# Moving the hidden-state loads from ScalarE's DMA queue to SyncE's, and four filler matmuls instead of two

## The chip, the cores and the metric

The kernel runs on the 8 cores of one Trainium2 chip, as the same program on each core, without communication between them. The metric is the device time in microseconds of the slowest core. Engines are named as in the profile: PE is TensorE, DVE is VectorE, ACT is ScalarE, POOL is GpSimd, SP is SyncE; PEld are PE's weight loads. An engine name with a q behind it (ACTq, SPq) is that engine's sequencer, for instance while it issues a DMA.

## What is computed

A transformer layer of attention and a quantized feed-forward part on 32 sequences of 2048 tokens and width 1024, four sequences for each core:

```python
def act_quant(x):
    scale = 127.0 / jnp.clip(jnp.max(jnp.abs(x), axis=-1, keepdims=True), 1e-05)
    return jnp.clip(jnp.round(x * scale), -128, 127) / scale
...
def _L0_ffn_ref(x, w1, conv_w, conv_b, w2):      # hidden width 4096
    h = bit_linear(x, w1)                        # act_quant(x) @ ternary(w1).T
    h = depthwise_conv1d(h.transpose(0, 2, 1), conv_w, conv_b)   # 3 taps along the tokens
    h = jax.nn.silu(h.transpose(0, 2, 1))
    return bit_linear(h, w2)                     # act_quant(h) @ ternary(w2).T
...
x = _layernorm(x + _L0_attn_ref(x, Wq, Wk, Wv), axis=-1)         # causal attention, one head
x = _layernorm(x + _L0_ffn_ref(x, w1, conv_w, conv_b, w2), axis=-1)
```

The second `bit_linear` needs the largest absolute value of each token over all 4096 hidden channels before it can round any of them. So the hidden state h is written to HBM while its maxima are gathered, and read back later.

## The kernel before

Each core works through its four sequences one after the other. A sequence has these stages: load and transpose x; the V projection; attention in four blocks of 512 tokens; the first half of the feed-forward part ("FFN1"), cut into 128 chunks (4 token blocks j times 32 channel tiles c); and the second half ("FFN2"), four blocks of 512 tokens, each with 32 chunks c and an end part.

Instructions are written in program order into one stream for each engine; an engine starts an instruction only when all those before it in its stream have started, and waits on semaphores where the code says so. Such a wait holds whatever stands behind it in that stream. DMAs are written by three helpers: `Sy` puts a DMA into SP's stream, `Gp` into POOL's, `Sd` into ACT's. The common helper `_dma` deals the DMAs of one stream to four "lanes" (semaphores) in turn, and adds a wait to each DMA: the one before it in the same lane must have landed. So at most four DMAs of one stream are in flight, and a stream's DMA number k is not issued before number k-4 has landed.

**FFN1.** `emit_chunk` loads the weight tile `w1s` (SP), does 16 one-column matmuls (L498 and L503, the two border tokens) and 8 matmuls of 512 columns (L510) on PE, and then DVE copies and scales the results out of PSUM into `hsf` (L516, L519, L527). The border matmuls of the next chunk wait for L519 of this one, its main matmuls for L527. `chunk_mid` does the convolution and SiLU, `chunk_back` writes h to `hs_s` and updates the maxima (`maxb`, `negb`). Some chunks are slipped in between attention work by `pump`; the rest run as a tail after attention, by `pump(10 ** 9, dummies=True)`. Only in this tail, two filler matmuls of 64 columns (L523, L525, result never read) follow the main matmuls of each chunk in PE's stream.

**FFN2.** At the head of block j a chain of small steps turns the maxima into the scales `sbc` (the last step is the ACT copy L953). For each chunk c then:

- `ldh(c)` loads h from `hs_s` into `hsr[c % 3]`. It waits until `f2_tt(c - 3)` has read the buffer. It stands in ACT's stream.
- `f2_tt(c)` (DVE, L973) multiplies by `sbc`, `f2_magic(c)` (DVE, L978) rounds, `f2_i32(c)` (DVE, L986) converts, `f2_cast(c)` (ACT, L994) writes `hq`, of which there are three buffers.
- `f2_mm(c)` loads the weight tile `w2s[c % 4]` (SP, L1006) once the matmuls of chunk c-4 are done, and does 8 matmuls of 512 columns (PE, L1014), accumulating over c in all eight PSUM banks.

The order in which they are written decides what stands behind what:

```python
            for cp in range(3):
                ldh(cp)
            for c in range(NH + 1):
                if c < NH:
                    f2_tt(c)
                    f2_magic(c)
                    if c + 3 < NH:
                        ldh(c + 3)
                if c >= 1:
                    f2_i32(c - 1)
                    f2_cast(c - 1)
                    f2_mm(c - 1)
```

In the end part ACT and DVE split the eight banks into high and low halves (L1035, L1038), PE transposes them, DVE adds the residual `x2rd` (L1075, loaded by SP at L1054), and after the layer norm POOL stores `y` (L1097). SP's stream holds, in this order, the w2s loads of block j, its four x2rd loads, and the w2s loads of block j+1.

Of the kernel before, what the change touches and what calls it, by code (L numbers as in the profile page):

```python
# [29 lines left out]
class Prog:  # L30
# [18 lines left out]

    def op(self, eng, fn, waits=(), inc=None, inc_n=1):  # L50
        w = [(s, v) for (s, v) in self._flat(waits) if v > 0]
        if eng in self.AUTO and (inc is None or inc == self.AUTO[eng]):
            sem = self.AUTO[eng]
            idx = self.cnt.get(sem, 0) + 1
            self.cnt[sem] = idx
            chain = (sem, idx - 1)
            self.streams[eng].append((fn, w, sem, 1, chain))
            return (sem, idx)
        self.streams[eng].append((fn, w, inc, inc_n, None))
        if inc is not None:  # L60
            self.cnt[inc] = self.cnt.get(inc, 0) + inc_n
            return (inc, self.cnt[inc])
        return None
# [31 lines left out]
def build_program(T=2048, nseq=4, phases=5):  # L95
# [36 lines left out]
    identB = SB("identB", [128, 128], BF16)  # L132
# [50 lines left out]
    def AT(name, shape, dt, off):  # L183
# [45 lines left out]
               for k in range(4)]  # L229
# [22 lines left out]
    ps = es.enter_context(nc.psum_tensor("ps", [128, 4096], F32))  # L252

    NLANE = 4
    sem_names = (["tv", "vv", "sv"]
                 + [f"ld{i}" for i in range(NLANE)]
                 + [f"gd{i}" for i in range(NLANE)]
                 + [f"sd{i}" for i in range(NLANE)])
    sems = {n: es.enter_context(nc.semaphore(n)) for n in sem_names}
    P = Prog()  # L260
    _rr = {"ld": 0, "gd": 0, "sd": 0}

    def _dma(eng, queue, fn, waits):
        lane = f"{queue}{_rr[queue] % NLANE}"
        _rr[queue] += 1
        w = list(waits) + [P.tok(lane)]
        return P.op(eng, fn, w, lane, 16)

    def Sy(fn, waits=()):
        return _dma("sync", "ld", fn, waits)  # L270

    def Gp(fn, waits=()):
        return _dma("gpsimd", "gd", fn, waits)

    def Sd(fn, waits=()):
        return _dma("scalar", "sd", fn, waits)

    def Qtok(queue):
        return [P.tok(f"{queue}{i}") for i in range(NLANE)]

    def Tn(fn, waits=(), inc=None):
        return P.op("tensor", fn, waits, inc, 1)
# [39 lines left out]
    for i_m in range(ND):  # L322
        for jh in range(2):
# [3 lines left out]
            for ce in range(ND):  # L327
# [4 lines left out]
                    start=(ce == 0), stop=(ce == ND - 1)),  # L332
                    waits=wmb if ce == 0 else ())
# [7 lines left out]
               waits=[P.tok("tv")])  # L341
# [144 lines left out]
    def emit_chunk(jj, c, dummies):  # L486
        gc = gck[0]
        gck[0] += 1
        t0 = jj * 512
        stw = w1stage[gc % 3]  # L490
        hsb = hsf[gc % 2]
        ct = ctmp[gc % 2]
        wld = [g_hmm[gc - 3]] if gc >= 3 else [t_prologue_g]
        tld = Sy(lambda e, c=c, stw=stw: e.dma_start(stw[:, :], d_w1q[c]), waits=wld)
        ul = unlock_tok[jj]
        whL = [tld, ul, g_evLR.get(gc - 1)]
        for cd in range(ND):
            Tn(lambda e, cd=cd, stw=stw, t0=t0: e.matmul(  # L498
                ps[:, 3072:3073], stw[:, cd * 128:(cd + 1) * 128],
                XQ2T[:, cd * XQW + t0: cd * XQW + t0 + 1],  # L500
                start=(cd == 0), stop=(cd == ND - 1)), waits=whL if cd == 0 else ())
        for cd in range(ND):
            Tn(lambda e, cd=cd, stw=stw, t0=t0: e.matmul(  # L503
                ps[:, 3073:3074], stw[:, cd * 128:(cd + 1) * 128],
                XQ2T[:, cd * XQW + t0 + 513: cd * XQW + t0 + 514],
                start=(cd == 0), stop=(cd == ND - 1)))
        t_hLR = P.inc_last("tensor", "tv")
        wmn = [g_mainev.get(gc - 1)] if gc >= 1 else [tld, ul]
        for cd in range(ND):
            Tn(lambda e, cd=cd, stw=stw, t0=t0: e.matmul(  # L510
                ps[:, 3584:4096], stw[:, cd * 128:(cd + 1) * 128],
                XQ2T[:, cd * XQW + 1 + t0: cd * XQW + 1 + t0 + 512],
                start=(cd == 0), stop=(cd == ND - 1)),
                waits=wmn if cd == 0 else ())
        g_hmm[gc] = P.inc_last("tensor", "tv")
        Vc(lambda e, hsb=hsb, t0=t0: e.tensor_tensor(  # L516
            hsb[:, 0:1], ps[:, 3072:3073], sxinvb[:, t0:t0 + 1], OP.mult),
            waits=[t_hLR, ul, g_conv.get(gc - 2)])
        g_evLR[gc] = Vc(lambda e, hsb=hsb, t0=t0: e.tensor_tensor(  # L519
            hsb[:, 513:514], ps[:, 3073:3074], sxinvb[:, t0 + 513:t0 + 514],  # L520
            OP.mult))
        if dummies:
            Tn(lambda e: e.matmul(ps[0:64, 0:64], identB[:, 0:64], identB[:, 0:64],  # L523
                                  start=True, stop=True))
            Tn(lambda e: e.matmul(ps[0:64, 0:64], identB[:, 0:64], identB[:, 0:64],  # L525
                                  start=True, stop=True))
        g_mainev[gc] = Vc(lambda e, hsb=hsb, t0=t0: e.tensor_tensor(  # L527
            hsb[:, 1:513], ps[:, 3584:4096], sxinvb[:, 1 + t0:1 + t0 + 512],
            OP.mult), waits=[g_hmm[gc]])
        return (jj, c, gc)  # L530
# [66 lines left out]
    for s in range(nseq if phases >= 2 else 0):  # L597
# [8 lines left out]
        for i in range(NT):  # L606
# [11 lines left out]
            if i >= 2:  # L618
                wc.append(t_evac[i - 2])
            t_cast[i] = Vc(lambda e, stx=stx, stb=stb: e.tensor_copy(stb[:, :], stx[:, :]),  # L620
                           waits=wc, inc="vv")
# [4 lines left out]
            for cd in range(ND):  # L626
# [3 lines left out]
                    start=True, stop=True), waits=wts if cd == 0 else ())  # L630
# [4 lines left out]
                waits=[tt], inc="vv")  # L635
# [3 lines left out]
        if phases < 3:  # L639
            continue  # L640
        tldv = Sy(lambda e: e.dma_start(Wv2[:, :], d_wvb),
                  waits=([t_mdone, t_wvst] if s == 0 else
                         [t_prev_t, t_prev_g, t_mdone]))
        t_kdone = P.tok("sv")
        tve = {}
        for i in range(NT):
# [6 lines left out]
            for cd in range(ND):  # L653
                for h in range(2):
# [4 lines left out]
                        start=(cd == 0), stop=(cd == ND - 1)),  # L659
                        waits=wts if (cd == 0 and h == 0) else ())  # L660
# [38 lines left out]
        for sb in range(NBL):  # L699
            for ce in range(ND):  # L700
# [4 lines left out]
                for cd in range(ND):  # L705
# [4 lines left out]
                        start=(cd == 0), stop=(cd == ND - 1)),  # L710
                        waits=wts if cd == 0 else ())
# [3 lines left out]
                    waits=[tt])  # L715
# [5 lines left out]
            for iq in range(4):  # L721
                i = sb * 4 + iq
# [5 lines left out]
                for ce in range(ND):  # L728
                    for kb in range(nkb):
# [5 lines left out]
                            start=(ce == 0), stop=(ce == ND - 1)),  # L735
                            waits=wts if (ce == 0 and kb == 0) else ())
                t_s = P.inc_last("tensor", "tv")
                pro_pump(1)
                if phases >= 5 and iq % 2 == 1:
# [11 lines left out]
                    waits=[tv_m])  # L751
                tv_li = Vc(lambda e: e.reciprocal(linv[:, :], lsum[:, :]),
                           waits=[t_exp[i]])
# [139 lines left out]
        t_ldh = {}  # L893
# [4 lines left out]
        for j in range(NBL):  # L898
# [57 lines left out]
            def ldh(c):  # L956
                hb = hsr[c % 3]
                wlh = [t_spill_h[(j, c)]]
                if (j, c - 3) in t_tt2:
                    wlh.append(t_tt2[(j, c - 3)])  # L960
                elif j > 0:
                    wlh.append(t_tt2[(j - 1, NH - 3 + c)])
                else:
                    wlh.append(t_attn_t)
                    wlh.append(t_prologue_g)
                t_ldh[(j, c)] = Sd(lambda e, j=j, c=c, hb=hb: e.dma_start(
                    hb[:, :], d_hs[j, c]), waits=wlh)

            def f2_tt(c):
# [131 lines left out]
    pro_drain()  # L1101

    P.op("gpsimd", lambda e: e.nop(), waits=Qtok("gd"))
    P.op("sync", lambda e: e.nop(), waits=Qtok("ld") + Qtok("sd"))

    with es:
        with nc.Block() as block:
# [57 lines left out]
```

How the kernel before makes its waits and increments, by code:

```python
            def body(e, recs=recs, eng=eng):  # L79
                seen = {}
                for fn, waits, inc, inc_n, chain in recs:
                    for s, v in waits:
                        if v > seen.get(s, 0):
                            e.wait_ge(sems[s], v)
                            seen[s] = v
                    ins = fn(e)
                    if chain is not None and chain[1] > seen.get(chain[0], 0):
                        ins._wait_ge(sems[chain[0]], chain[1])
                        seen[chain[0]] = chain[1]
                    if inc is not None:
                        ins.then_inc(sems[inc], inc_n)
```

## Time and profile before

| | us |
|---|---|
| median of 2 runs | 6655.19 (6643.06 to 6667.33) |
| the profiled execution | 6619.96 |
| span of its slowest core (core 4) | 6618.3 |
| spans of the 8 cores | 6593.2 to 6618.3 |
| mean granted clock of PE | 0.76 of full, on every core |
| PE busy / DVE busy / ACT busy | 3917.3 / 3949.3 / 2082.2 |

The profiled execution is 35 us shorter than the median of the timed runs; durations below are of that execution. The profile's page gives sums over the span; the views of the trace give single instructions (start, duration, engine, line, output and inputs), what ended an engine's idle time before an instruction (in square brackets), and busy times, granted clock and DMA traffic of a stretch. Times of a row are microseconds from the span's start. Rows marked x with a number are merged from so many instructions, and their duration reaches from the first one's start to the last one's end.

### The profile page before, as it was taken

What the parts mean: (1) busy time and instruction counts of PE and PEld (TensorE: products, weight loads), DVE (VectorE), ACT (ScalarE), POOL (GpSimd) and SP (SyncE); (2) the same over time, 40 slices, a digit from 0 to 9 for tenths busy, and PEclk for the clock granted to TensorE, in tenths of its full rate; (3) what the DMA queues carried; (4) which work ended last, traced back from release to release, by engine and by line L of the source; (5) the groups of instructions that cost most, each with busy time, mean ns of one, the idle gap of its engine ahead of it and who ended that gap; (6) DMA issues with size and microseconds to landing.
All of it is one profiled execution on the core that took longest, in us unless ns stands there. A gap on an engine that the chain in (4) does not pass through costs nothing.

```text
span 6618.3 us, 77507 instructions; the slowest of 8 cores (6593.2 to 6618.3 us)
## 1 busy us (share of the span) xinstructions
PE 3917.3 (59%) x24062; PEld 1865.7 (28%) x24504; DVE 3949.3 (60%) x7242; ACT 2082.2 (31%) x2857; POOL 407.9 (6%) x712
## 2 busy tenths in 40 slices
PE   2412566675656566676565466576655656667575
PEld 1101223232323223233233223233322322333232
DVE  2135465796662356698663356589665256579775
ACT  1313333333331233333331233333332233333333
POOL 0111000110000000010000000011000000011000
PEclk7756778787877778788787678777776877878786
DMA  7535122335752122234563122133655022233565
GB/s 198 175 125 164 63 86 77 99 125 162 205 176 76 48 76 83 83 125 155 181 209 110 46 78 82 61 120 123 200 183 191 26 69 80 77 99 125 164 213 162
DMA packets 331396, 810.77 MB, mean 123 GB/s; under 512 B 40304, under 2 KB 40560, under 8 KB 326256
## 3 DMA queue, kind: packets, MB, share of 16 engines
q1 hardware_dynamic: 181296, 411.45, 20.6%
q0 software_dynamic: 75968, 260.09, 10.8%
q10 hardware_dynamic: 73728, 134.25, 6.8%
q8 instruction: 204, 3.34, 0.2%
q14 instruction: 200, 1.64, 0.1%
HBM read 591.72 MB, written 220.20 MB: 123 GB/s over the span
## 4 chain that ended last, share of the span: by engine, by line
DVE 40%; PE 24%; DMA 15%; ACT 12%; issue 7%; DVEq 0%; ACTq 0%; SPq 0%; POOLq 0%; POOL 0%
DMA hsr<-hs_s 7%; PE ps L773 5%; PE ps L510 5%; DVE ctmp L542 5%; DVE ctmp L539 5%; PE ps L1014 5%; DVE hsf L527 4%; DVE negb L567 3%; DVE maxb L564 3%; PE ps L655 3%; DMA pstgh<-w2t 2%; DVE qtmp L973 2%; DMA hs_s<-ctmp 2%; PE ps L706 2%; PE ps L731 2%
## 5 line engine op out<-in xcount | busy, mean ns | idle before, releaser
L510 PE MATMUL ps<-XQ2T,w1s 128*128 128x512 bf16 x3844 | 1182.9, 457 | 150.2 <-DVE hsf L527 135.1
L1014 PE MATMUL ps<-hq,w2s 128*128 128x512 bf16 x4004 | 948.5, 392 | 166.4 <-DVE qtmp L978 91.6
L545 ACT ACTIVATE ctmp<-ctmp,convb 128x512 f32<-128x512 f32 x512 | 369.7, 722 | 979.5 <-DVE ctmp L542 979.1
L1014 PEld LDWEIGHTS ps<-hq,w2s 128*128 128x128 bf16 x4096 | 395.0, 100 | 716.2 <-issue 338.4
L510 PEld LDWEIGHTS ps<-XQ2T,w1s 128*128 128x128 bf16 x4096 | 411.1, 109 | 630.2 <-issue 372.1
L994 ACT ACTIVATE hq<-qi,noffbc 128x512 bf16<-128x512 int32 x512 | 369.6, 722 | 682.0 <-DVE qi L986 570.0
L536 ACT ACTIVATE ctmp<-hsf,convw 128x512 f32<-128x512 f32 x512 | 369.5, 722 | 336.3 <-DVE negb L567 229.6
L973 DVE TENSOR_TENSOR qtmp<-hsr,sbc 128x512 f32<-128x512 f32 x512 | 354.4, 692 | 195.5 <-DMA hsr<-hs_s 158.4
L498 PE MATMUL ps<-XQ2T,w1s 128*128 128x1 bf16 x4096 | 177.4, 164 | 480.6 <-DVE hsf L519 476.2
L539 DVE SCALAR_TENSOR_TENSOR ctmp<-hsf,convw,ctmp 128x512 f32<-128x512 f32 x512 | 384.5, 751 | 86.8 <-ACT ctmp L536 71.7
L527 DVE TENSOR_TENSOR hsf<-ps,sxinvb 128x512 f32<-128x512 f32 x512 | 354.7, 693 | 97.9 <-PE ps L510 82.9
L554 POOL DMA_DIRECT2D hs_s<-ctmp x512 | 276.7, 540 | 2031.1 <-ACT ctmp L545 1959.5
L786 DVE SCALAR_TENSOR_TENSOR t1buf<-ps,linv,xstage 128x1024 f32<-128x1024 f32 x64 | 82.1, 1283 | 526.2 <-PE ps L773 526.2
L542 DVE SCALAR_TENSOR_TENSOR ctmp<-hsf,convw,ctmp 128x512 f32<-128x512 f32 x512 | 384.8, 752 | 18.2
L773 PE MATMUL ps<-Vtm,PT 128*128 128x512 bf16 x1036 | 337.4, 489 | 67.1 <-ACT PT L763 61.2
L564 DVE TENSOR_TENSOR maxb<-maxb,ctmp 128x512 f32<-128x512 f32 x496 | 343.0, 692 | 17.1
L567 DVE SCALAR_TENSOR_TENSOR negb<-ctmp,negb 128x512 f32<-128x512 f32 x496 | 343.1, 692 | 16.9
L655 PE MATMUL ps<-Wv,XTq 128*128 128x512 bf16 x1000 | 247.3, 410 | 135.8 <-ACT Vtm L662 117.4
L498 PEld LDWEIGHTS ps<-XQ2T,w1s 128*128 128x128 bf16 x4096 | 152.6, 99 | 612.3 <-issue 598.2
L731 PE MATMUL ps<-XTq,QT 128*128 128x512 bf16 (+3 forms) x1268 | 273.2, 374 | 71.5 <-ACT ctmp L545 38.0
L758 PE MATMUL ps<-identB,Pbuf 128*128 128x128 bf16 x544 | 72.5, 303 | 398.4 <-ACT Pbuf L748 347.6
L706 PE MATMUL ps<-XTq,WqB 128*128 128x512 bf16 x1016 | 245.1, 393 | 94.3 <-ACT pternh L422 77.9
(175 smaller groups left out, 4628.8 us busy)
## 6 DMA issues: line engine op xcount, KB each, us to landing
w1s<-w1q_s SPq DMA_DIRECT2D x512, 256.0 KB, 2.7
hs_s<-ctmp POOLq DMA_DIRECT2D x512, 256.0 KB, 2.7
w2s<-w2q_s SPq DMA_DIRECT2D x512, 256.0 KB, 4.5
hsr<-hs_s ACTq DMA_DIRECT2D x512, 256.0 KB, 4.4
xstage<-x SPq DMA_DIRECT2D x128, 512.0 KB, 4.1
pstgh<-w1t SPq DMA_DIRECT2D x32, 1024.0 KB, 7.6
pstgh<-w2t POOLq DMA_DIRECT2D x32, 1024.0 KB, 6.5
x_s<-x2buf POOLq DMA_DIRECT2D x64, 512.0 KB, 2.9
```

The source lines that it names most:

```text
L510: Tn(lambda e, cd=cd, stw=stw, t0=t0: e.matmul(ps[:, 3584:4096], stw[:, cd * 128:(cd + 1) * 128], XQ2T[:, cd * XQW + 1 + t0: cd * XQW + 1 ...
L527: g_mainev[gc] = Vc(lambda e, hsb=hsb, t0=t0: e.tensor_tensor(hsb[:, 1:513], ps[:, 3584:4096], sxinvb[:, 1 + t0:1 + t0 + 512], OP.mult), w ...
L539: Vc(lambda e, ct=ct, hsb=hsb, c=c: e.scalar_tensor_tensor(ct[:, :], hsb[:, 1:513], convw[:, 3 * c + 1:3 * c + 2], ct[:, :], OP.mult, OP.a ...
L542: g_conv[gc] = Vc(lambda e, ct=ct, hsb=hsb, c=c: e.scalar_tensor_tensor(ct[:, :], hsb[:, 2:514], convw[:, 3 * c + 2:3 * c + 3], ct[:, :], ...
L564: Vc(lambda e, mb=mb, ct=ct: e.tensor_tensor(mb[:, :], mb[:, :], ct[:, :], OP.max), waits=[t_sil])
L567: lambda e, nb=nb, ct=ct: e.scalar_tensor_tensor(nb[:, :], ct[:, :], -1.0, nb[:, :], OP.mult, OP.max))
L655: Tn(lambda e, i=i, cd=cd, h=h, pc=pc: e.matmul(ps[:, pc + h * 512: pc + (h + 1) * 512], XTq[:, cd * T + i * 128: cd * T + (i + 1) * 128], ...
L706: Tn(lambda e, ce=ce, cd=cd, sb=sb, pc=pc: e.matmul(ps[:, pc:pc + 512], WqB[:, cd * D + ce * 128: cd * D + ce * 128 + 128], XTq[:, cd * T ...
L731: Tn(lambda e, ce=ce, kb=kb, Jk=Jk, iq=iq: e.matmul(ps[:, kb * KJ: kb * KJ + Jk], QT[:, ce * 512 + iq * 128: ce * 512 + (iq + 1) * 128], X ...
L773: Tn(lambda e, c=c, h=h, i=i: e.matmul(ps[:, 2048 + h * 512: 2048 + (h + 1) * 512], PT[:, c * 128:(c + 1) * 128], Vtm[:, c * D + h * 512: ...
L973: t_tt2[(j, c)] = Vc(lambda e, c=c: e.tensor_tensor(qtmp[c % 2][:, :], hsr[c % 3][:, :], sbc[:, :], OP.mult), waits=whq)
L1014: Tn(lambda e, c=c, ce=ce: e.matmul(ps[:, ce * 512:(ce + 1) * 512], w2stage[c % 4][:, ce * 128:(ce + 1) * 128], hqb[c % 3][:, :], start=(c ...
```

## The change

- The load of h (`ldh`) is written with `Sy` in place of `Sd`: it moves from ACT's stream to SP's, at the same place in the program order, and takes part in SP's four lanes. The helper `Sd` and its four semaphores are gone.
- In the tail of FFN1 four filler matmuls follow each chunk instead of two.
- `op` now treats every instruction of DVE and ACT alike, which changes nothing for those that are left.

```diff
@@ def op
-        if eng in self.AUTO and (inc is None or inc == self.AUTO[eng]):
+        if eng in self.AUTO:
             sem = self.AUTO[eng]
+            assert inc is None or inc == sem
@@ build_program
-                 + [f"gd{i}" for i in range(NLANE)]
-                 + [f"sd{i}" for i in range(NLANE)])
+                 + [f"gd{i}" for i in range(NLANE)])
-    _rr = {"ld": 0, "gd": 0, "sd": 0}
+    _rr = {"ld": 0, "gd": 0}
-    def Sd(fn, waits=()):
-        return _dma("scalar", "sd", fn, waits)
@@ emit_chunk
         if dummies:
-            Tn(lambda e: e.matmul(ps[0:64, 0:64], identB[:, 0:64], identB[:, 0:64],
-                                  start=True, stop=True))
-            Tn(lambda e: e.matmul(ps[0:64, 0:64], identB[:, 0:64], identB[:, 0:64],
-                                  start=True, stop=True))
+            for _ in range(4):
+                Tn(lambda e: e.matmul(ps[0:64, 0:64], identB[:, 0:64],
+                                      identB[:, 0:64], start=True, stop=True))
@@ ldh
-                t_ldh[(j, c)] = Sd(lambda e, j=j, c=c, hb=hb: e.dma_start(
+                t_ldh[(j, c)] = Sy(lambda e, j=j, c=c, hb=hb: e.dma_start(
                     hb[:, :], d_hs[j, c]), waits=wlh)
@@ end of program
-    P.op("sync", lambda e: e.nop(), waits=Qtok("ld") + Qtok("sd"))
+    P.op("sync", lambda e: e.nop(), waits=Qtok("ld"))
```

## Rows read from the trace of the kernel before

**Rows 1.** The page, part 1: busy times and their shares of the span.
```profile
PE 3917.3 (59%) x24062; PEld 1865.7 (28%) x24504; DVE 3949.3 (60%) x7242; ACT 2082.2 (31%) x2857; POOL 407.9 (6%) x712
```

**Rows 2.** The page, parts 5 and 6: L973, then the w2s and h loads (last: us to landing).
```profile
L973 DVE TENSOR_TENSOR qtmp<-hsr,sbc 128x512 f32<-128x512 f32 x512 | 354.4, 692 | 195.5 <-DMA hsr<-hs_s 158.4
...
w2s<-w2q_s SPq DMA_DIRECT2D x512, 256.0 KB, 4.5
hsr<-hs_s ACTq DMA_DIRECT2D x512, 256.0 KB, 4.4
```

**Rows 3.** Windows: us, busy PE, PEld, DVE, ACT, POOL, PEclk, DMA share, GB/s.
```profile
3203.70:3213.60 9.90, 3.14 (x8) 1.31 (x10) 6.66 (x13) 2.17 (x3) 0.00 (x0) 0.50 0.58 175
3213.60:3271.20 57.60, 55.03 (x244) 22.90 (x246) 42.81 (x84) 20.97 (x30) 0.00 (x0) 1.00 0.84 262
```

**Rows 4.** Timeline of the same FFN2 block (second sequence, j = 1): its start.
```profile
3203.10 0.58 ACT L953 COPY sbc<-ps 128x512 f32<-128x512 f32 x1 [1.63 <-PE ps L947]
...
3205.96 0.69 DVE L973 TENSOR_TENSOR qtmp<-hsr,sbc 128x512 f32<-128x512 f32 x1 [4.11 <-DMA hsr<-hs_s]
...
3207.22 0.69 DVE L973 TENSOR_TENSOR qtmp<-hsr,sbc 128x512 f32<-128x512 f32 x1
...
3209.00 0.72 ACT L994 ACTIVATE hq<-qi,noffbc 128x512 bf16<-128x512 int32 x1 [5.31 <-DMA hsr<-hs_s]
...
3210.05 0.14 PEld L1014 LDWEIGHTS ps<-hq,w2s 128*128 128x128 bf16 x2 [7.30 <-issue]
```

**Rows 5.** Timeline of the block's end: the last L973, and ACT behind the last matmul.
```profile
3264.66 0.69 DVE L973 TENSOR_TENSOR qtmp<-hsr,sbc 128x512 f32<-128x512 f32 x1 [0.81 <-DMA hsr<-hs_s]
...
3271.17 1.82 ACT L1035 CAST hi<-ps 128x512 bf16<-128x512 f32 x3 [3.20 <-PE ps L1014]
```

**Rows 6.** Timeline of SP's queue: ahead of the block, and in it at full clock.
```profile
3156.92 22.09 SPq L1054 DMA_DIRECT2D x2rd<-x_s  x4
...
3213.78 5.51 SPq L1006 DMA_DIRECT2D w2s<-w2q_s  x4
```

**Rows 7.** Timeline of two chunk steps within the block.
```profile
3240.89 0.69 DVE L973 TENSOR_TENSOR qtmp<-hsr,sbc 128x512 f32<-128x512 f32 x1 [0.24 <-DMA hsr<-hs_s]
...
3241.72 0.33 ACTq L966 DMA_DIRECT2D hsr<-hs_s  x1
...
3242.69 0.69 DVE L973 TENSOR_TENSOR qtmp<-hsr,sbc 128x512 f32<-128x512 f32 x1
3242.73 0.72 ACT L994 ACTIVATE hq<-qi,noffbc 128x512 bf16<-128x512 int32 x1 [1.21 <-DVE qi L986]
```

**Rows 8.** Line L966, the block's first three h loads, issued 3203.2 to 3204.1.
```profile
DMA to landing us min/median/max: 2.7/3.0/3.7
```

**Rows 9.** Waits over the whole span: in total, times, longest.
```profile
DVE outb L1075 <- DMA y<-outb: 51.9, 13, 5.4
```

**Rows 10.** Tile w2s over the whole span: its matmuls' waits for its loads.
```profile
  DMA w2s<-w2q_s: 17.0, 36
```

**Rows 11.** Windows of the FFN1 tail: all of sequence 2, two stretches of sequence 1.
```profile
2799.80:3074.30 274.50, 197.94 (x1660) 93.59 (x1692) 252.22 (x456) 94.03 (x131) 35.12 (x65) 0.82 0.39 127
...
1401.10:1411.30 10.20, 6.72 (x73) 3.62 (x74) 9.64 (x17) 2.89 (x4) 1.08 (x2) 1.00 0.49 154
1411.30:1418.10 6.80, 5.46 (x37) 2.23 (x37) 6.01 (x13) 2.89 (x4) 1.08 (x2) 0.50 0.25 80
```

**Rows 12.** Line L527 in the tail of sequence 2: DVE's waits for PE.
```profile
  PE ps L510: 6.1, 14
```

**Rows 13.** Timeline of a tail chunk at half clock, around the fillers.
```profile
1417.74 0.24 PE L525 MATMUL ps<-identB 128*64 128x64 bf16 x1
...
1417.84 0.69 DVE L527 TENSOR_TENSOR hsf<-ps,sxinvb 128x512 f32<-128x512 f32 x1 [0.41 <-PE ps L510]
...
1418.15 0.34 PE L503 MATMUL ps<-XQ2T,w1s 128*128 128x1 bf16 x8
1418.68 1.89 PE L510 MATMUL ps<-XQ2T,w1s 128*128 128x512 bf16 x8 [0.20 <-DVE hsf L527]
```

## The prediction

> **What bounds the kernel now.** I read part 1 of the page first: DVE and PE are each busy for three fifths of the span [rows 1], so no engine is full over the whole, and each stage has to be read alone. The change touches two: FFN2 (16 blocks) and the FFN1 tail (4 tails).
>
> In FFN2, parts 5 and 6 show that DVE's L973 waits 158.4 us in all for the h loads, and that h loads and w2s loads take 4.4 and 4.5 us to land [rows 2], while three h loads issued on an almost idle set of DMA engines land in 2.7 to 3.7 us [rows 8]. The windows of one block (3203.7 to 3271.2, 67.5 us) show the rest: 9.9 us at half clock and 57.6 us at full clock, PE busy 3.1 and 55.0 us, DMA share 0.84, 262 GB/s [rows 3]. Three things lie close together there. PE needs 1.73 us for a chunk at full clock (four w2s issues, each released by a finished chunk, in 5.51 - 0.32 = 5.19 us [rows 6]). DVE needs 1.80 (3240.89 to 3242.69 [rows 7]). What is reached is (3264.66 - 3205.96) / 31 = 1.89 [rows 4, 5]. From the first weight load on PE (3210.05) to the split of the banks (3271.17) are 61.1 us, of which PE is busy 58.2 [rows 3 to 5]: the block is nearly PE's, behind a slow start.
>
> The FFN1 tail: DVE is busy 252.2 of 274.5 us, PE 197.9 [rows 11]. DVE is the bound; it waits for PE's main matmuls for only 6.1 us in a tail, in 14 chunks [rows 12], those at half clock.
>
> **Edit 1, start of a block (a gain for DVE, little of one for PE).** Before, the first three h loads stand in ACT's stream behind the copy of `sbc`, so L973 starts 3205.96 - 3203.68 = 2.28 us after it [rows 4]. In SP's stream they stand behind the x2rd loads of the block before, whose last is issued by 3179.0 [rows 6], 24 us earlier; they will have landed. L973 then starts within 0.1 us: -2.2 us for DVE in each block, 16 times. PE does not get that. `w2s(0)` was loaded over 20 us ahead; now it stands in SP's stream behind h(3) and h(4), which wait for L973 of chunks 0 and 1. The second L973 ends 1.26 + 0.69 = 1.95 us after the first one's start [rows 4]; with the 0.1 us ahead of that and 0.5 us for the issue of h(4) (three issues start within 0.9 us [rows 8]), `w2s(0)` goes out 2.6 us after `sbc`. Landing takes 2.7 to 4.4 us [rows 2, 8]; with only two h loads beside it I take 3.3. PE starts at 5.9 us after `sbc`, before at 6.4 (3210.05 - 3203.68): -0.5 us, between -1.1 and +0.6.
>
> **Edit 1, the pace.** The two streams had up to 3 h loads (three buffers) and 4 w2s loads in flight. Now both kinds alternate in one stream with four lanes, so h(c+4) waits for the landing of h(c+2), and w2s(c) for that of w2s(c-2): two chunks in a landing time L and 0.1 us. At L = 4.4 that is 2.25 us a chunk; at L = 3.5 it equals DVE's 1.80. How does L move? Now 2 loads x 4.4 / 1.89 = 4.7 are in flight on average; if the same bytes flow with at most four, L is 4 x 1.89 / 2 = 3.8. No row shows FFN2 with four in flight. The bounds are 2.7 [rows 8], where DVE's 1.80 decides, and 4.4 [rows 2]. I take 3.75, since a load's wait beyond the 2.7 us is mostly for the loads ahead of it: (3.75 + 0.1) / 2 = 1.93 against 1.89, over 31 steps +1.2 us. Bounds: 31 x (1.80 - 1.89) = -2.8 and 31 x (2.25 - 1.89) = +11.2.
>
> **Edit 1, the weights are late.** `w2s(c)` now waits behind h(c+4), which waits for L973 of chunk c+1. It lands 0.55 + 3.75 = 4.3 us after that L973's end; `hq(c)` is ready 1.87 us after it (3241.58 to 3243.45 [rows 7]). So PE trails `hq` by 2.4 us, where it waited for w2s only 17.0 us in all before [rows 10]. This does not stop DVE: ACT's cast of chunk c needs the `hq` buffer of c-3, three steps (5.6 us) old. It shows at the end. Before, 3264.66 + 0.69 = 3265.35 to 3271.17, 5.8 us, pass from the last L973 to the split [rows 5]. After it, counting from the L973 of chunk 28 (5.4 us earlier, the last with an h load behind it): 0.55 + 3.75 to w2s(27), 1.95 for its matmuls (eight of this size span 1.89 us [rows 13]), 0.1 + 3.75 for w2s(31), which takes the buffer of 27, and 1.95 again, less 5.4 = 6.65 us: +0.8 (L = 4.4: +2.1; L = 3.3: 0). And since PE has lost its store of four loaded tiles, every late landing now stops it; I add 1.0 us a block, between 0 and the whole lag of 2.4.
>
> The sum for a block: -2.2 + 1.2 + 0.8 + 1.0 = +0.8 us. Checked from PE's side: it starts 0.5 us earlier, has 58.2 us of work and idled 2.9 us; +0.8 means that it idles 4.2. Times 16: +13 us. PE's own work is the floor: 5.9 + 58.2 = 64.1 us, -3.4 a block, -54 in all. The ceiling is -2.2 + 11.2 + 2.1 = +11 a block, +177 in all.
>
> The 512 issues that leave ACT (0.33 us each [rows 7]) cost nothing before and bring nothing now: ACT is busy 23.1 of 67.5 us in the block. On SP two issues of about 0.5 us in 1.9 us fit. The y stores, for which L1075 waits 51.9 us in all [rows 9], met three w2s loads issued behind the last x2rd; now they meet three h loads of the same size: 0.
>
> The Trainium skill (DMA: Bandwidth & Descriptors, section "Issuing engines are not separate DMA queues") says that DMAs issued by different engines run on the same 16 DMA engines and that spreading them saves only the sequencer's issue time. By it alone edit 1 would be worth 0, the fourth case below; what it leaves out is the order within one stream, on which the terms above rest.
>
> **Edit 2.** 66 chunks a tail get two more fillers. At full clock PE waits for DVE between chunks, so they are hidden. At half clock the stretch from L525 (1417.74) to the end of L503 (1418.49) lies under L527, which ends at 1418.53, and L510 starts at 1418.68 [rows 13]. Two more fillers push L503 by 0.07 to 0.2 us, of which 0.04 to 0.19 is slack: 0 to 0.16 us in each of 4 x 14 chunks, up to +9 us; I take +2. Could they keep the clock up? Full for 10.2 us, half for 6.8 [rows 11], again and again, though PE is the busier in the half-clock stretch (5.46 of 6.80 us). If the clock stayed up, DVE's waits would go: 4 x 6.1 = -24 us [rows 12]. Two fillers add about 0.1 us of work to a 4.1 us chunk, so I expect no more than a trace of that. The Trainium skill (TensorE: Matmul & The Clock Gate, section "HAM oscillation — how this bites in real kernels") lays such swings to idle gaps of PE between bursts; by it fillers would help, and the sum would be -24 in place of +2.
>
> **Sum.** +13 + 2 = +15 us: 6620 becomes 6635. The median of the timed runs stands 35 us above that execution, so 6655 becomes **6670**.
>
> **The rivals.**
> - *The cap of four bites.* L stays at 4.4 (whatever stretches it is not the loads queued ahead). Then h waits for lanes, 2.25 us a chunk, 6655 + 177 + 2 = 6834. For it: a DMA share of 0.84 in the block. Against: 2.7 to 3.7 us for three at once. It passes 2% (133 us, 8.3 a block) once L is above 4.2.
> - *The start is a gain and the late weights are hidden.* L falls under 3.5, DVE runs at 1.80: down to PE's floor, -54, and with a steadier clock -24 more: 6655 - 54 = 6601, at best 6577. For it: PE idles only 2.9 us now, and L973 loses 158.4 us to loads.
> - *Faster by over 2%* would need more than 8 us a block, and PE's own work allows 3.4. Only a clock that rises at once in each block would add more.
> - *Nothing moves:* the same bytes on the same engines, start gained and end lost alike: 6655.
>
> **How the numbers follow.** Chances: my forecast (6640 to 6710) 0.55, the cap 0.13, the gain 0.15, nothing moves 0.15, over 2% faster 0.02. A part of the cap's cases, L between 4.0 and 4.2, is slower by less than 2%. The range leaves out about 1 in 10 on either side: 6600 to 6790. 2% is about what a measurement of this kernel tells from no change. Faster by over 2%: 0.03; within 2%: 0.85; slower by over 2%: 0.12.
>
> **What would show it.** The first L973 of a block within 0.2 us of the `sbc` copy's end; the first L1014 5.9 us behind it; h and w2s landing times of 3.7 to 3.8 us; L973 steps of 1.93 us; L1014 waiting for w2s loads far more than 17.0 us in all; 6.6 us from the last L973 to L1035. In the tails the same swings of the clock. It is wrong if landing times stay at 4.4 us, if SP's queue needs longer for an issue than ACT's 0.33 us, or if PE's new waits lengthen the stretch at half clock: PE works at half speed there, so each further microsecond costs up to half of one.

## The result, and the profile after

| | before | after |
|---|---|---|
| median of the timed runs, alternating | 6631.53 us (42 runs) | 6668.96 us (43 runs) |
| ratio, 95% interval | | 1.0061 [1.0046, 1.0077] |
| profiled execution, spans of the 8 cores | 6593.2 to 6618.3 | 6619.7 to 6667.4 |
| mean of the 8 spans | 6606.8 | 6647.0 |

The change costs 0.6%, about 40 us (31 to 51 by the interval; 40.2 by the means of the spans). In some executions the cores of one die (0 to 3 or 4 to 7) show a lower granted clock than the rest and take longer; below, only undisturbed dies are read, those whose four cores all show a granted clock of 0.756 or more.

The page of the changed kernel (core 2), parts 5 and 6: groups with busy time and mean ns, then the idle time before them by what ended it; then loads with the us to landing.

```profile
L1010 PE MATMUL ps<-hq,w2s 128*128 128x512 bf16 x4004 | 941.4, 389 | 222.3 <-DMA w2s<-w2q_s 138.9
L990 ACT ACTIVATE hq<-qi,noffbc 128x512 bf16<-128x512 int32 x512 | 369.6, 722 | 712.5 <-PE ps L1010 377.0
L969 DVE TENSOR_TENSOR qtmp<-hsr,sbc 128x512 f32<-128x512 f32 x512 | 354.3, 692 | 191.4 <-DMA hsr<-hs_s 126.1
...
hsr<-hs_s SPq DMA_DIRECT2D x512, 256.0 KB, 4.1
w2s<-w2q_s SPq DMA_DIRECT2D x512, 256.0 KB, 4.0
```

PE's FFN2 matmuls (L1014 before, L1010 now) waited for w2s loads 17.0 us in all [rows 10]; now it is 138.9. DVE's waits for h loads fell from 158.4 [rows 2] to 126.1 us, and both kinds of load land sooner, in 4.0 to 4.1 us instead of 4.4 to 4.5. ACT's wait for PE grew as well, from 69.8 to 377.0 us: the cast needs an `hq` buffer that PE has not yet read. That row before:

```profile
ACT hq L994 <- PE ps L1014: 69.8, 57, 2.2
```

The windows of the FFN2 block that answers to [rows 3] (second sequence, j = 1): us, busy PE, PEld, DVE, ACT, POOL, PEclk, DMA share, GB/s.

```profile
3228.20:3239.20 11.00, 3.44 (x9) 1.36 (x11) 9.12 (x18) 2.32 (x4) 0.00 (x0) 0.50 0.64 196
3239.20:3301.80 62.60, 54.60 (x243) 23.32 (x246) 41.03 (x80) 22.08 (x32) 0.00 (x0) 1.00 0.75 239
```

PE's work is the same (3.44 + 54.60 = 58.0 us, before 58.2). At full clock it is now spread over 62.6 us instead of 57.6, and the DMA share falls from 0.84 to 0.75: neither PE nor the DMA engines are fuller. PE waits for loads, and the loads are issued late. The timeline of that block's start, with SP's queue:

```profile
3227.58 0.59 ACT L949 COPY sbc<-ps 128x512 f32<-128x512 f32 x1 [1.62 <-PE ps L943]
3228.34 0.69 DVE L969 TENSOR_TENSOR qtmp<-hsr,sbc 128x512 f32<-128x512 f32 x1 [2.00 <-ACT sbc L949]
3229.16 1.60 SPq L962 DMA_DIRECT2D hsr<-hs_s  x2
3231.24 0.32 SPq L1002 DMA_DIRECT2D w2s<-w2q_s  x1
3235.76 1.06 PE L1010 MATMUL ps<-hq,w2s 128*128 128x512 bf16 x2 [8.27 <-ACT hq L990]
```

L969 starts 0.17 us behind the copy (before 2.28 [rows 4]). The first w2s load goes out behind h(3) and h(4), 3.07 us after the copy. PE's first matmul starts 7.6 us after the copy here, its first weight load 7.2 (6.4 on the mean of all blocks). SP's queue later in the same block:

```profile
3270.42 0.32 SPq L1002 DMA_DIRECT2D w2s<-w2q_s  x1
3271.03 0.32 SPq L962 DMA_DIRECT2D hsr<-hs_s  x1
3271.84 0.32 SPq L1002 DMA_DIRECT2D w2s<-w2q_s  x1
3272.53 0.32 SPq L962 DMA_DIRECT2D hsr<-hs_s  x1
3274.65 0.32 SPq L1002 DMA_DIRECT2D w2s<-w2q_s  x1
3275.28 0.32 SPq L962 DMA_DIRECT2D hsr<-hs_s  x1
3276.07 0.32 SPq L1002 DMA_DIRECT2D w2s<-w2q_s  x1
3276.70 0.32 SPq L962 DMA_DIRECT2D hsr<-hs_s  x1
3279.17 0.32 SPq L1002 DMA_DIRECT2D w2s<-w2q_s  x1
```

That is the pattern of the lanes: four issues close together, then a stop until the first of them has landed. From one w2s issue to the next but one are 3274.65 - 3270.42 = 4.23 and 3279.17 - 3274.65 = 4.52 us, a landing time (4.16 and 4.45 us for the first and third w2s load of these) and 0.07 us, for two chunks: 2.1 to 2.3 us a chunk, where PE needs 1.73. That holds for nearly all: of the w2s loads in the middle of a block (chunks 8 to 26, cores 0 to 3) 99% go out within 0.25 us of the landing of the fourth DMA before them in SP's stream, on the median 0.07 us behind it. Before, the issues followed PE's chunks, four in 5.51 us [rows 6]. PE in the same microseconds, then the block's last L969 and ACT's first L1031:

```profile
3270.48 3.61 PE L1010 MATMUL ps<-hq,w2s 128*128 128x512 bf16 x15 [0.41 <-DMA w2s<-w2q_s]
3274.71 3.61 PE L1010 MATMUL ps<-hq,w2s 128*128 128x512 bf16 x16 [0.62 <-DMA w2s<-w2q_s]
3279.23 2.97 PE L1010 MATMUL ps<-hq,w2s 128*128 128x512 bf16 x13 [0.91 <-DMA w2s<-w2q_s]
```

```profile
3290.51 0.69 DVE L969 TENSOR_TENSOR qtmp<-hsr,sbc 128x512 f32<-128x512 f32 x1 [0.87 <-DMA hsr<-hs_s]
...
3300.43 3.67 ACT L1031 CAST hi<-ps 128x512 bf16<-128x512 f32 x6 [4.45 <-PE ps L1010]
```

PE does two chunks, waits, does two chunks. At the end 3300.43 - 3291.20 = 9.2 us pass from the last L969 to the split, before 5.8 [rows 5].

All 16 blocks of the four cores of die 0, mean in us, worked out from the timelines: "first", "PE" and "block" count from the end of the `sbc` copy to the first multiplication with `sbc`, to PE's first weight load and to the split; "pace" is the mean step of that multiplication; "end" runs from its last to the split; "landing" is the median of h and of w2s loads; "end part" is from the split to the next block's first instruction. (one_stream_quiet is read on die 1.) The kernels below `after` are the experiments.

Kernels whose FFN2 is the same can differ by 0.7 (before and fill4_only) and even 1.4 us (after and move_only) in "block". The last column, "span", rests on more executions: it is the mean span of all undisturbed dies in all timed executions of a kernel, less the same mean of the kernel before in the same session on the same chip; it is good to 4 to 7 us (95%). The experiments ran in three sessions, each on a chip of its own (fill4_only to cap_2_2; lanes8 to lanes8_ahead with early_h_quiet; the others), and the kernel before came out there at 6594.8, 6595.0 and 6601.2 us, where its profiled execution in the first line has 6606.8. So "block" of an experiment is better compared with another experiment than with the first line: against that line it flatters by 0.4 to 0.8 us. For `after`, "span" is from the two profiled executions.

| kernel | first | PE | pace | end | block | landing h, w2s | end part | span |
|---|---|---|---|---|---|---|---|---|
| before | 2.3 | 6.5 | 1.92 | 5.8 | 68.4 | 4.3, 4.5 | 29.6 | 0 |
| after | 0.2 | 6.4 | 1.97 | 9.3 | 71.4 | 4.0, 4.0 | 29.7 | +40 |
| fill4_only | 2.3 | 6.5 | 1.90 | 5.9 | 67.7 | 4.3, 4.5 | 29.5 | -7 |
| move_only | 0.2 | 6.2 | 1.94 | 9.1 | 70.0 | 3.9, 3.8 | 29.7 | +41 |
| late_w2s | 2.3 | 8.7 | 2.01 | 8.1 | 73.4 | 4.7, 4.5 | 28.1 | +71 |
| cap_2_2 | 2.2 | 6.5 | 2.05 | 7.2 | 73.8 | 4.1, 4.2 | 29.5 | +96 |
| lanes8 | 0.2 | 6.3 | 1.85 | 8.8 | 67.1 | 4.2, 4.3 | 29.7 | -19 |
| w2s_ahead | 0.2 | 4.3 | 1.96 | 5.9 | 67.6 | 3.9, 3.9 | 29.7 | -1 |
| lanes8_ahead | 0.2 | 4.3 | 1.87 | 5.8 | 64.6 | 4.1, 4.2 | 29.6 | -51 |
| early_h | 0.2 | 4.3 | 1.91 | 5.8 | 65.8 | 4.4, 4.5 | 29.5 | -32 |
| early_h_quiet | 0.2 | 4.3 | 1.92 | 5.9 | 66.3 | 4.5, 4.5 | 28.2 | -48 |
| two_streams | 0.2 | 4.3 | 1.93 | 5.8 | 66.6 | 4.5, 4.5 | 29.5 | -18 |
| one_stream_quiet | 0.2 | 4.3 | 1.90 | 5.9 | 65.5 | 4.2, 4.4 | 28.2 | -65 |
| one_stream_5buf | 0.2 | 4.3 | 1.78 | 7.1 | 63.0 | 4.5, 4.2 | 28.3 | -89 |

Over both dies a block goes from 68.5 to 71.2 us: 16 x 2.7 = 43 us, all of the difference (40.2 by the spans). The FFN1 tails did not change: from the first to the last filler, the four tails of a core sum to 1102.8 us before and 1101.5 us after, on the mean of the eight cores.

### The profile page after: what moved, and what is told of

Read it like the earlier page. It is cut to its first block, busy times and chain, and to the rows that moved or that the text cites. A ratio compares the mean times of both kernels' runs of the same rounds, so it can differ in the third digit from the quotient of the medians.

```text
span 6667.4 us, 78995 instructions; the slowest of 8 cores (6619.7 to 6667.4 us)
## 1 busy us (share of the span) xinstructions
PE 3932.7 (59%) x24590; PEld 1884.0 (28%) x25032; DVE 3947.9 (59%) x7242; ACT 2082.6 (31%) x2857; POOL 405.5 (6%) x712
## 4 chain that ended last, share of the span: by engine, by line
DVE 37%; PE 22%; DMA 20%; ACT 12%; issue 6%; DVEq 0%; SPq 0%; ACTq 0%; POOLq 0%; POOL 0%
DMA w2s<-w2q_s 12%; PE ps L769 5%; PE ps L507 5%; DVE ctmp L538 5%; DVE ctmp L535 5%; DVE hsf L523 4%; DVE negb L563 4%; DVE maxb L560 4%; PE ps L1010 3%; PE ps L651 3%; DMA pstgh<-w2t 2%; PE ps L702 2%; DMA pstgh<-w1t 1%; DMA y<-outb 1%; PE ps L727 1%
## 5 line engine op out<-in xcount | busy, mean ns | idle before, releaser
L1010 PE MATMUL ps<-hq,w2s 128*128 128x512 bf16 x4004 | 941.4, 389 | 222.3 <-DMA w2s<-w2q_s 138.9
L1010 PEld LDWEIGHTS ps<-hq,w2s 128*128 128x128 bf16 x4096 | 394.5, 99 | 765.5 <-issue 354.5
L990 ACT ACTIVATE hq<-qi,noffbc 128x512 bf16<-128x512 int32 x512 | 369.6, 722 | 712.5 <-PE ps L1010 377.0
L969 DVE TENSOR_TENSOR qtmp<-hsr,sbc 128x512 f32<-128x512 f32 x512 | 354.3, 692 | 191.4 <-DMA hsr<-hs_s 126.1
```

What stands on the lines that cost most here:

```text
L990: t_hq[(j, c)] = Sc(lambda e, c=c: e.activation(hqb[c % 3][:, :], qi32[c % 2][:, :], AF.Identity, bias=noffbc[:, 0:1]), waits=w)
L1010: Tn(lambda e, c=c, ce=ce: e.matmul(ps[:, ce * 512:(ce + 1) * 512], w2stage[c % 4][:, ce * 128:(ce + 1) * 128], hqb[c % 3][:, :], start=(c ...
```

## Experiments

### Which of the two edits: fill4_only and move_only

fill4_only is the kernel before with the second edit alone; move_only is the changed kernel with two fillers.

```diff
 # fill4_only, against before
-            Tn(...)   # twice
+            for _ in range(4):
+                Tn(...)
```

> The kernel before with four fillers a tail chunk, the loads left where they were. The prediction: +2 us, between -24 (the fillers hold the clock up) and +9 (they delay L510 at half clock). If the fillers carried the measured change of about +40 us, this kernel would show 1.006; by the two theories on the moved loads it shows 1.000 within 0.001, and the tails keep their length of about 275 us.

Measured: 1.0004 [0.994, 1.0067], spans 6574.2 to 6603.4 us, tails 1101.2 us a core. DVE's waits in front of L526 (L527 before) over the whole span, core 0 of before, then of fill4_only:

```profile
L527 DVE TENSOR_TENSOR hsf<-ps,sxinvb 128x512 f32<-128x512 f32 x512 | 354.7, 693 | 99.5 <-PE ps L510 84.8 <-DVE hsf L519 0.5
```

```profile
L526 DVE TENSOR_TENSOR hsf<-ps,sxinvb 128x512 f32<-128x512 f32 x512 | 354.7, 693 | 98.0 <-PE ps L510 83.0 <-DVE hsf L519 0.5
```

The ratio alone could hide 40 us either way; the tails settle it. With two fillers on the same chip they take 1101.0 (move_only), 1101.3 (late_w2s) and 1100.2 us (cap_2_2), so four fillers bring neither the up to 9 us of cost nor the 24 us of gain. The granted clock of the tails of cores 0, 2 and 4 is 0.80 to 0.82 before and 0.80 to 0.83 here. By "span" the kernel is 7 us faster; that does not lie in the tails, and its cause is open.

> The changed kernel with two fillers as before: only the loads are moved. Both theories on the loads: all of the change, ratio 1.006 (+35 to +50 us), last L973 to the split of the banks 9.4 us. If the fillers had their share, less.

Measured: 1.0042 [0.9992, 1.0093]; block 70.0 us, "end" 9.1 us. The first edit alone shows every trait of the changed kernel. The interval does not separate 1.0042 from 1.0061, nor by itself from 1. "span" does: +41 us, within 5 us, with two fillers.

### Which part of the first edit: late_w2s and cap_2_2

Theory A: the order of the stream makes the weights late. Theory B: the four lanes make them slow. Each kernel puts one of the two into the kernel before, whose streams stay as they were.

```diff
 # late_w2s
                     wst = [t_attn_t, t_prologue_g]
+                if (j, c + 1) in t_tt2:
+                    wst = wst + [t_tt2[(j, c + 1)]]
 # cap_2_2
+                wlh.append(t_ldh.get((j, c - 2)))
                 t_ldh[(j, c)] = Sd(...)
+                wst = wst + [t_w2l.get((j, c - 2))]
-                t_w2st = Sy(...)
+                t_w2st = t_w2l[(j, c)] = Sy(...)
```

> The kernel before, h loads in ACT's stream, but each w2s load of chunk c also waits for L973 of chunk c+1, as it does in the changed kernel through the order of the stream. No load waits for a lane any more than before. Theory A (order: the weights are late because they stand behind h loads that wait for DVE): PE trails from the start, the block's end grows from 5.85 to about 9 us, and since the 2.2 us gained at the start are missing here, a block is 4 to 5 us longer: +65 to +80 us, 1.010 to 1.012. Theory B (lanes: at most two w2s loads in flight, 2 chunks in a landing time): only the first matmuls of a block are late, w2s(c) still lands within DVE's and ACT's next steps; end of block 6 to 7 us, a block 0.5 to 1.5 us longer: +8 to +24 us, 1.001 to 1.004.

> The kernel before, order and streams as they were, but each h load of chunk c waits for the landing of h(c-2) and each w2s load for that of w2s(c-2): two and two in flight at most, four in all, as in the changed kernel's lanes. Theory A (order): nothing to speak of, 0 to +10 us, since w2s is still issued as soon as its buffer is free. Theory B (lanes): landing times fall from 4.4 to about 4.0 us, the w2s stream goes at (4.0 + 0.1) / 2 = 2.05 us a chunk against PE's 1.73, PE falls behind by some 3 us in a block; +2.5 to +5 us a block, +40 to +80 us, 1.006 to 1.012.

Measured: late_w2s 1.0105 [1.0046, 1.0164], block 73.4 us (+5.0); cap_2_2 1.0185 [1.0087, 1.0283] from four timed runs, block 73.8 us (+5.4). By "span" they cost 71 and 96 us, 1.011 and 1.015. So A was right on late_w2s and B on cap_2_2 (it had up to 80 us), and each was wrong on the other. PE's and DVE's groups, core 0 of late_w2s and then of cap_2_2:

```profile
L1016 PE MATMUL ps<-hq,w2s 128*128 128x512 bf16 x4004 | 942.5, 389 | 244.7 <-DMA w2s<-w2q_s 105.2 <-DVE qi L986 68.8 <-ACT hq L994 54.4
L973 DVE TENSOR_TENSOR qtmp<-hsr,sbc 128x512 f32<-128x512 f32 x512 | 354.5, 692 | 235.7 <-DMA hsr<-hs_s 205.3 <-DVE qi L986 1.4
```

```profile
L1017 PE MATMUL ps<-hq,w2s 128*128 128x512 bf16 x4004 | 945.1, 389 | 251.9 <-DMA w2s<-w2q_s 112.9 <-DVE qi L988 64.4 <-DVE qtmp L980 46.2
L975 DVE TENSOR_TENSOR qtmp<-hsr,sbc 128x512 f32<-128x512 f32 x512 | 354.5, 692 | 263.5 <-DMA hsr<-hs_s 234.1 <-DVE qi L988 1.3
```

Each limit alone makes PE wait over 100 us for weights, where it waited 17.7 us on this core of the kernel before. Both limits are real, and the open question became whether they add.

### Taking the limits out of the changed kernel: lanes8, w2s_ahead, lanes8_ahead

```diff
 # lanes8: eight lanes in SP's stream
+    LANES = {"ld": 8, "gd": 4}
-        lane = f"{queue}{_rr[queue] % NLANE}"
+        lane = f"{queue}{_rr[queue] % LANES[queue]}"
 # w2s_ahead: f2_w(c) is the w2s load, taken out of f2_mm(c)
             for cp in range(3):
                 ldh(cp)
+            for cp in range(2):
+                f2_w(cp)
...
                     if c + 3 < NH:
                         ldh(c + 3)
+                    if 1 <= c < NH - 1:
+                        f2_w(c + 1)
```

> The changed kernel with eight lanes for SP's stream: up to eight DMAs in flight, order unchanged (w2s(c) still behind h(c+4)). Theory C (each limit alone is enough, they overlap): still like late_w2s but with the early start, block 70 to 71 us against 71.2 in the changed kernel, 1.003 to 1.006 of the kernel before. Theory D (the two limits add, half each): block near 69 us, 1.000 to 1.002. w2s must then wait for no lane: landing times back up at 4.4 to 4.7 us.

> The changed kernel with each w2s load two chunks earlier in SP's stream (w2s(0), w2s(1) behind the first three h loads, then w2s(c+1) behind h(c+3)); four lanes as they are. First matmuls start as soon as hq is there, 4.2 us behind sbc instead of 6.4. Theory C: from there on the lanes set the pace, (L + 0.1) / 2 = 2.05 us a chunk, PE falls behind, block 69 to 71 us, 1.001 to 1.006. Theory D: half of the loss is gone, block near 68.5 us, 1.000.

> Both of the last two edits in one: eight lanes, and w2s loads two chunks earlier. Theories C and D alike: neither limit is left, only the early start: PE starts 4.2 to 4.5 us behind sbc, pace about 1.9, last L973 to the split 5.9 to 6.2 us, block 66 to 67 us, 16 x -2.2 = -35 us against the kernel before, 0.994 to 0.997. If the block stays above 68.5 us, a single DMA stream has a cost of its own that neither theory has.

Measured: 0.9966 [0.9937, 0.9995], 0.9995 [0.9961, 1.0028] and 0.9914 [0.9858, 0.9971]; blocks 67.1, 67.6 and 64.6 us. The changed kernel and move_only have 71.4 and 70.0, on the mean 70.7. From 64.6, the lanes alone add 3.0 (w2s_ahead), the order alone 2.5 (lanes8), both 6.1. By "span", from -51 us, the lanes alone add 50, the order alone 32, both 92 (move_only). Theory C, that one limit hides the other, falls; D, that they add, holds. D's own numbers were too timid: both single kernels came out 1 to 2 us a block better than it gave. PE's group on core 0 of lanes8, w2s_ahead and lanes8_ahead, and L969 of the last:

```profile
L1011 PE MATMUL ps<-hq,w2s 128*128 128x512 bf16 x4004 | 927.4, 388 | 157.8 <-DVE qtmp L975 42.3 <-DMA w2s<-w2q_s 35.8 <-ACT hq L991 34.4
```

```profile
L1014 PE MATMUL ps<-hq,w2s 128*128 128x512 bf16 x4004 | 942.5, 387 | 151.9 <-DVE qtmp L974 59.1 <-DMA w2s<-w2q_s 42.8 <-ACT hq L990 34.6
```

```profile
L1015 PE MATMUL ps<-hq,w2s 128*128 128x512 bf16 x4004 | 934.4, 388 | 108.2 <-DVE qtmp L975 59.1 <-ACT hq L991 27.1 <-DMA w2s<-w2q_s 9.1
L970 DVE TENSOR_TENSOR qtmp<-hsr,sbc 128x512 f32<-128x512 f32 x512 | 354.4, 692 | 128.0 <-DMA hsr<-hs_s 53.8 <-ACT sbc L950 32.1 <-DVE qi L983 0.9
```

The waits for w2s go from 142.6 us on this core of the changed kernel to 35.8, 42.8 and 9.1. In the one-stream kernels the table tells the two limits apart: the order sets when PE starts (6.3 or 4.3) and how long the end takes (9 or 5.9), the lanes set the pace (1.96 or 1.86). PE's idle time from its first weight load of a block to its last matmul (mean of the blocks of die 0) says it from the other side: 2.9 us before, 5.6 in the changed kernel, 3.8 with the lanes' limit alone (w2s_ahead), 2.3 with the order alone (lanes8), 1.3 with neither. So the lanes cost idle time within the block, and the order costs mostly the later start.

The last kernel is faster than the kernel before by 3.8 us a block (3.2 by "span"), where the early start accounts for 2.0 to 2.6. Something else helps it; the next runs ask what.

### One stream or two: early_h, early_h_quiet, two_streams

```diff
 # early_h, against before: ldh and its first three calls stand ahead of the chain that makes sbc
+            for cp in range(3):
+                ldh(cp)
             Vc(lambda e, j=j: e.tensor_tensor(
                 mxf[:, :], maxbufs[j][:, :], negbufs[j][:, :], OP.max),
 # early_h_quiet, besides
-                    wst = [t_f2mm[(j - 1, NH - 4 + c)]]
+                    wst = [t_f2mm[(j - 1, NH - 4 + c)], t_y2T_ev[j * 4 - 1]]
 # two_streams, against early_h: the calls of f2_w as in w2s_ahead, and
+                if c >= 2:
+                    wst = wst + [t_tt2[(j, min(c - 1, NH - 4))]]
```

> The kernel before (h loads in ACT's stream) with two edits: the first three h loads of a block are written ahead of the chain that makes sbc, and the w2s loads that were issued during the end part of the block before wait for its last L1075. From the first: L973 starts 0.1 us behind sbc, PE 4.2 us behind it instead of 6.5, block 66 to 66.5 us, -35 us. From the second: the y stores no longer share the DMA engines with a burst of loads, the end part falls from 29.6 to 28.0 us as in late_w2s, 12 x -1.6 = -19 us. Together -54 us, 0.992. If PE's clock rises later because of it, or the DMA engines are the true bound, less: 0.995.

> The kernel before with one edit: the first three h loads of a block are written ahead of the chain that makes sbc, still in ACT's stream. It takes the two edits of early_h_quiet apart. L973 starts 0.1 us behind sbc, PE 4.3 us behind it, block 66 us as there (-2.4 us, 16 times, -38 us), and the end part is back at 29.6 us, because four w2s loads are again issued while the y stores run: 0.994. If the end part stays at 28.2 us, the burst of w2s loads is not what delays the y stores.

> The schedule of lanes8_ahead in two streams: h loads in ACT's stream (the first three early), w2s(c+1) in SP's stream, released by the same L973 of chunk c that stands ahead of it there, two tiles early at a block's start. Theory E (one stream makes the same loads land sooner than two that take turns on the DMA engines): landing 4.4 to 4.6 us as in the kernels with two streams, pace 1.91, block 66 us. Theory F (the shorter landings of lanes8_ahead come from when the w2s loads are issued, not from the stream): landing 4.1 us, pace 1.87, block 64.7 us, as there.

Measured: early_h_quiet 0.9894 [0.9837, 0.9952] (from two timed runs), early_h 0.9963 [0.9939, 0.9987], two_streams 0.998 [0.9962, 0.9997]. The first L976 starts 0.17 us behind `sbc` in all three and a block takes 65.8 us in early_h: the early start alone, with the weights still ahead, gives 2.6 us a block (2.0 by "span"). The end part is 29.5 us in early_h and 28.2 in early_h_quiet, and "span" differs by 16 us, 12 x 1.3: the burst of w2s loads does delay the y stores. The instruction that waits for them, core 0 of early_h, then of early_h_quiet:

```profile
L1076 DVE SCALAR_TENSOR_TENSOR outb<-ps,scale2tm,x2rd 128x1024 f32<-128x1024 f32 x64 | 82.2, 1284 | 101.7 <-DMA y<-outb 52.9 <-PE ps L1066 36.0 <-DMA w2s<-w2q_s 10.1
```

```profile
L1076 DVE SCALAR_TENSOR_TENSOR outb<-ps,scale2tm,x2rd 128x1024 f32<-128x1024 f32 x64 | 82.2, 1284 | 87.5 <-DMA y<-outb 48.8 <-PE ps L1066 36.0
```

The 10.1 us put down to w2s loads are waits for y stores too: in all 16 blocks of either kernel the third L1076 starts 0.10 us after the landing of the block's first y store, and 7.5 and 6.4 us (medians) after that of its x2rd load. That store lands in 6.0 us (median) in early_h and in 4.9 in early_h_quiet.

two_streams and lanes8_ahead issue the same loads at nearly the same moments: in the middle of a block an h load goes out 0.13 us behind the end of the multiplication that releases it in both, the w2s load that belongs to it 1.03 and 0.74 us behind it (medians, die 0). What differs is the stream of the h loads, and with it the lanes (four for each stream against eight for one; neither holds an h load back). Theory E is borne out in both of its numbers: h loads land in 4.5 against 4.1 us, and a block takes 66.6 against 64.6 us, 2.0 us by "span" too (-18 and -51 us). The two kernels ran on different chips, and the second has four fillers; one_stream_quiet below ran on the chip of two_streams, and its h loads land in 4.2 us. The landing times of w2s on core 0 of two_streams, then of lanes8_ahead:

```profile
DMA to landing us min/median/max: 2.5/4.5/7.2
```

```profile
DMA to landing us min/median/max: 2.5/4.1/8.6
```

What in the DMA engines makes the difference was not tried.

### Beyond both kernels: one_stream_quiet and one_stream_5buf

one_stream_quiet is lanes8_ahead with `t_y2T_ev[j * 4 - 1]` added to the waits of a block's first h loads; one_stream_5buf has, besides, five h buffers, the calls `ldh(c + 5)` in place of `ldh(c + 3)`, twelve lanes, and waits for the attention stage before the first loads of a sequence.

> lanes8_ahead, and the loads of a block's start (three h, then two w2s) wait for the last L1075 of the block before. Block 64.7 us as there; end part 28.1 instead of 29.6 us, 12 times -1.5 = -18 us; the loads have 10 us (the chain that makes sbc) to land, so nothing is lost. -35 - 25 - 18: 0.988 of the kernel before.

> one_stream_quiet with five h buffers instead of three and twelve lanes. L973 should wait for h loads no more: pace 1.80 (DVE's own), down from 1.87. PE's work is the floor: 4.3 + 58.2 = 62.5 us; block 62.8 to 63.5 us, another -20 to -30 us, 0.984 to 0.986. If the DMA engines are the bound, landing times rise to 5 us and more, and the pace stays at 1.85.

Measured: 0.9937 [0.9896, 0.9978] and 0.988 [0.9851, 0.9909]. one_stream_quiet has the short end part (28.2 us). Its ratio is no better than the 0.9914 of lanes8_ahead and its profiled execution no shorter, but against the kernel before on its own chip it gains 65 us by "span", where lanes8_ahead gains 51: 14 of the 18 us expected, within 6. Its block, 65.5 us against 64.6, is within the scatter. With five buffers the pace is 1.78 and the block 63.0 us; the ratio is from two timed runs, "span" (-89 us, 0.987) from five dies. Core 0:

```profile
L1020 PE MATMUL ps<-hq,w2s 128*128 128x512 bf16 x4096 | 924.2, 388 | 88.6 <-ACT hq L996 64.7 <-DVE qtmp L980 15.6 <-DMA w2s<-w2q_s 7.8
L975 DVE TENSOR_TENSOR qtmp<-hsr,sbc 128x512 f32<-128x512 f32 x512 | 354.5, 692 | 83.4 <-ACT sbc L952 32.1 <-DVE qi L988 0.9
```

L975 waits for no load any more, and PE idles 88.6 us in all, most of it before a block's first matmul (16 x 4.3 = 69 us): a block is PE's work and its start. This kernel is the fastest of all, 1.2% below the kernel before and by the two ratios 1.8% below the changed one.

## Why the prediction was right, and what was off in it

The time (6668.96) lies within the range and by the forecast of 6670, and the direction and the cause (the order of the stream and its lanes) were right. That it lies so close is partly chance: the forecast was +15 us on a median of 6655, the measured change is +40 us on a median of 6631.5, more than twice as much.

1. *The start of a block, for DVE: -2.2 us.* Right: 2.3 to 0.2.
2. *PE's start at 5.9 instead of 6.4, -0.5 us.* In the right direction, but the gain was smaller: 6.4 against 6.5 on the mean. w2s(0) went out 2.7 us after `sbc` on the mean of die 0, not 2.6, and needed 3.4 us to land, not 3.3; the block shown, with 3.07 and 3.9 us, is one of the late ones.
3. *The pace, +1.2 us a block from landing times of 3.75 us.* The size is nearly right: 1.97 against 1.92 is +1.5. It is partly chance: the landing time is 4.0, and by the prediction's own formula (4.0 + 0.1) / 2 = 2.05, which would be +4.0; DVE loses less to the lanes than the formula has it. The cap of four does shorten landings, as the sum of bytes in flight said, and less than in proportion.
4. *The late weights, +0.8 and +1.0 us.* This is the term that was mis-sized. "End" grew by 3.5 us (5.8 to 9.3), not by 1.8, and PE idles 5.6 us in a block, before 2.9; the prediction had 4.2. I let the lanes act on the h loads, where DVE's 1.80 gives them slack, and for the weights only on the last two loads of a block. But w2s loads go through the same lanes at the same two chunks a landing time, and PE needs a tile every 1.73 us. The lag of w2s does not stay at 2.4 us: from chunk 9 to 27 w2s(c) lands 2.9 to 3.3 us behind the end of its cast (mean of die 0; 2.2 at chunk 0). Nor are the casts on time, though the prediction counted on an `hq` buffer that had been free for steps: they end 5.1 us behind their L969 (before 3.8), since ACT waits for PE. That DVE is not stopped by this was right: its L982 waits 6.6 us in all for the casts. The experiments give 2.5 us a block to the order and 3.0 to the lanes, 6.1 to both.
5. *A gain that was not in the sum.* A single stream lands the same loads sooner than two (4.1 against 4.5 us, 2.0 us a block). It hides a part of the loss. The sum for a block, from the runs: -2.6 for the early start (early_h), +0.8 for w2s loads issued two tiles ahead instead of four (two_streams against early_h; 0.9 by "span"), -2.0 for the single stream, +6.1 for both limits (with the changed kernel and move_only taken together): +2.3. Each term is the difference of two neighbours in one chain of kernels from before to after, so that the sum comes out is no check; what the chain gives is the split. By "span" it reads -2.0, +0.9, -2.0, +5.7.
6. *Fillers: +2 us, between -24 and +9.* Right to within what can be seen: tails 1.3 us shorter. The clock still swings in them (a mean of 0.80 to 0.82 in each tail of cores 0, 2 and 4, before and after).
7. *The y stores: 0.* Right: the end part stays at 29.6 to 29.7 us, and late_w2s, early_h_quiet and one_stream_quiet show that 1.4 us of each come from whatever loads are issued beside the stores.

Of the rivals, the cap that bites was the nearest to what happened, in a milder form: it bit the weights above all (h loads go out 0.88 us behind the end of the L969 that releases them, before 0.13, medians of die 0), and landing times fell instead of staying at 4.4 us. That nothing moves, which is what the Trainium skill's rule gives by itself (DMA: Bandwidth & Descriptors, section "Issuing engines are not separate DMA queues"), does not hold here in two ways: the order in one stream and the helper's limit on it cost 40 us, more than the early start gives, and two_streams against lanes8_ahead shows that the number of streams matters to landing times as well. By the Trainium skill (TensorE: Matmul & The Clock Gate, section "HAM oscillation — how this bites in real kernels"), which lays swings of the clock to PE's waits between bursts of matmuls, more work in PE's gaps should have held the clock; fill4_only doubles the fillers, and DVE waits for L510 83.0 us where it waited 84.8.

## What to carry to other kernels

A DMA that is moved to another engine's stream takes the waits of everything ahead of it and hands its own wait to everything behind: look for the transfer that was prefetched behind it, and ask what its new neighbour waits for. If a helper limits the transfers in flight by stream, merging two streams halves that limit for each; compare chunks in flight / landing time with the fastest consumer, here PE at 1.73 us, not with the one that the moved load feeds. One stream with enough lanes, and the prefetched kind written ahead of the demand kind, beat both kernels here.

## What the runs showed of the hardware that I had not expected

- The same loads (256 KB each, about 250 to 260 GB/s) issued at nearly the same moments land in 4.1 us from one stream (lanes8_ahead) and in 4.5 us from two (two_streams).
- With a limit of four in flight landing times fall to 3.8 to 4.2 us (move_only, cap_2_2), not to the 2.7 to 3.7 us of [rows 8]. What keeps them there was not tried.
- Doubling the filler matmuls in a DVE-bound loop (fill4_only) left PE's swings between full and half clock as they were: a mean granted clock of 0.80 to 0.83 in the tails, before 0.80 to 0.82.
